# Moving z to token rows by VectorE block transposes and a DRAM round trip, in a two-stage transformer and mixture-of-experts kernel

## Chip, cores and metric

One core of one Trainium2 chip. The metric is the device time of the program in microseconds (us), the median of several runs; smaller is better.

## What is computed

Eight sequences x of 512 tokens by 256 channels go through four layers of a block, are added to the input and normalised, and then go through a gated mixture of eight experts with another residual and normalisation. All in fp32.

```python
def block(h, p):
    r = _retention(h, wk)
    m = r @ w1 + b1
    a, gate = jnp.split(m, 2, axis=-1)
    m = a * jax.nn.silu(gate) @ w2 + b2
    m = _groupnorm1(m, gg, gb)
    y = m + h
    f = jax.nn.gelu(y @ wf1 + bf1_, approximate=False) @ wf2 + bf2_
    return (_layernorm(f + y, lg, lb), None)
x = _layernorm(x + _L0_attn_ref(x, ...), axis=-1)
x = _layernorm(x + _L0_ffn_ref(x, ...), axis=-1)
```

The sum f + y, before its layernorm, is what the kernel calls z.

## The kernel before

**Work and stages.** The first stage is the four layers: 4 layers times 4 pairs of sequences give 16 steps. In a step two sequences, A and B, are in two slots with buffers and four PSUM banks each. The second stage (experts) follows from about 1060 us on and is not touched.

**Layout.** Most tensors of a sequence lie transposed, with channels on partitions: two chunks (c = 0, 1) of 128 channels by 512 tokens. The layernorm needs rows of tokens: four blocks of 128 tokens by 256 channels. fp32 products are done as three matmuls of a high half and a low half (mm3); ScalarE (ACT) rounds the high half from PSUM or SBUF, and VectorE (DVE) subtracts it for the low half. So a matmul phase is followed by the chain ACT high, DVE low, and the next matmul phase waits for the low half.

**Order.** The order of work on each engine is written out by hand in the functions `body`. The two slots are half a step apart: `body` of step `now` does A's and B's attention of this step, and in between the rest of B's, and the end of A's, of the step `before`. On TensorE (PE) the order is: A's `transpose_h`; B's `gated_projection`; A's `project_t`; `transpose_z(A)` (line 1945, eight transposes of 128x128 of y into two banks); B's `out_projection`; A's `scores`, with B's one-column `group_moments` (L1908) between; `retain(A)`; B's `up_projection` (first chunk L1922 and L1925); `transpose_r(A)`; projections and down projections; `project_t(B)`; `group_moments(A)`; `transpose_z(B)`; `scores(B)`; `up_projection(A)`; `retain(B)`; and so on.

**z.** DVE's `residual` (L1319) adds the down projection to y, in place: y is z then, channels on partitions. PE's `transpose_z` brings it to token rows in PSUM, ACT's `keep_z` (L923, two instructions) copies it to the SBUF tile z. DVE takes the statistics (`layernorm_stats`, L1327, and `layernorm_var`, L1336 to L1339), GpSimd (POOL) the inverse root (L661), ACT normalises (L936), POOL applies gain and bias (L388, L395) into h_out. The next user is `store_h` on the SP queue, which stores h_out to DRAM (L460) for the next layer; `load_h` (L456) loads it four steps later, and so h_in comes back through DRAM anyway.

**Chains around the change.** B's `scores` wait for both chunks of `low_t` (L1188, tu_sp from PSUM). The `group_moments` feed `groupnorm_var` (L1281), POOL's inverse root (L656) and `groupnorm_out`: gained (L1292), summed (L1297, writes y), ACT's `high_y` (L902), DVE's `low_y` (L1188, ry_sp), and then `up_projection`. B's `out_projection` waits for `low_u` (L1188, tu_sp from tmp), chunk c outer and chunk k inner. DVE's end of `body` is: `low_p(B)`, statistics of B's z, two `divide` (L1233 to L1237), `low_r(B)` (ry_sp from PSUM), which the first matmul of the next step's `gated_projection(B)` needs. All DMAs of this stage are issued by SP, in order, each behind its waits.

```python
def transpose_z(s, at, first=0):
    pe.wait_ge(z_ready[s], at.base + U)
    for k in range(TB):
        for c in range(DC):
            to = (k % 2) * D + c * P
            ins = nc.tensor.transpose(bank(s, first + k // 2)[:, to:to + P], y[s][:, c, cols(k)], ident[:, :])
```

Of the kernel before, what the change touches and what calls it, by code (L numbers as in the profile page):

```python
# [21 lines left out]
F32 = mybir.dt.float32  # L22
# [5 lines left out]
P = 128  # L28
EPS = 1e-5
# [21 lines left out]
def network(nc, x, xT, WkqvT, Wm1, Wm2, Wf1, Wf2, layer_cols, ln_g, ln_b,  # L51
            Wr, br, W1, W2, expert_cols, score_floor, out, h_store, folded, gate_rows, prepared):
# [30 lines left out]
    h_v = h_store.rearrange("i s (k p) d -> i s p k d", p=P)  # L83

# [20 lines left out]
    with ExitStack() as ctx:  # L105
# [146 lines left out]

        held = sem("held")
# [9 lines left out]
        def split_count(name, layer):  # L263
            return layer * len(SPANS) + list(SPANS).index(name) + 1

# [15 lines left out]
        zT_psum, z_kept, h_new = sems("zT_psum"), sems("z_kept"), sems("h_new")  # L281
# [23 lines left out]
        end_shift, end_half = sem("end_shift"), sem("end_half")  # L305

# [97 lines left out]
        def _(sp):  # L404
# [56 lines left out]

            def step(it, load, seam=None):
# [59 lines left out]
            for s in range(SLOTS):  # L522
                sp.sem_inc(h_stored[s], DMA)
            load_part(0, 0, kq_loaded)
# [298 lines left out]
        def _(act):  # L823
            for s in range(SLOTS):
                act.sem_inc(z_kept[s], U)
# [93 lines left out]
            def keep_z(s, at):  # L919
                act.wait_ge(h_new[s], at.base + U)  # L920
                for i in range(2):
                    act.wait_ge(zT_psum[s], at.base + 2 * i + 2)
                    nc.scalar.activation(z[s][:, 2 * i:2 * i + 2, :].rearrange("p k d -> p (k d)"), bank(s, i),  # L923
                                         ACT.Copy).then_inc(z_kept[s], 2)

            def keep_z_end():
                for i in range(2):
                    act.wait_ge(zT_psum[B_], LAST_STEP.base + 2 * i + 2)
                    nc.scalar.activation(z_end[:, 2 * i:2 * i + 2, :].rearrange("p k d -> p (k d)"), bank(B_, 2 + i),
                                         ACT.Copy).then_inc(z_kept[B_], 2)  # L930
# [89 lines left out]
            def body(now, before, seam, last=False, entry=False):  # L1020
# [13 lines left out]
                if before:  # L1034
                    keep_z(A_, before)
                else:
# [42 lines left out]
                if before:  # L1079
                    keep_z(B_, before)  # L1080
                else:
# [37 lines left out]
            keep_z(A_, LAST_STEP)  # L1119
# [12 lines left out]
            for w in range(QUADS):  # L1132
# [7 lines left out]
                if w == 0:  # L1140
                    keep_z_end()
# [38 lines left out]
        def _(dve):  # L1180
# [58 lines left out]
            def gated(s, at, c):  # L1239
                dve.wait_ge(m_psum[s], at.base + 2 * c + 2)  # L1240
# [76 lines left out]
            def residual(s, at, c):  # L1317
# [3 lines left out]
                    op0=ALU.add, op1=ALU.add).then_inc(z_ready[s], 2)  # L1321
# [262 lines left out]
            def body(now, before, seam, last=False, entry=False):  # L1584
# [3 lines left out]
                if seam:  # L1588
                    dve.wait_ge(z_ready[A_], before.base + U)
# [9 lines left out]
                if before:  # L1599
                    gated_products(B_, before)  # L1600
# [32 lines left out]
                if seam:  # L1633
                    dve.wait_ge(z_ready[B_], before.base + U)
# [5 lines left out]
                groupnorm_out(A_, now)  # L1640
                low_p(B_, now, range(TB))
                if before:
# [3 lines left out]
                for half in range(2):  # L1646
                    divide(B_, now, half)
# [124 lines left out]
        def _(pe):  # L1772
# [65 lines left out]
            def scores(s, at, blocks):  # L1838
                for b in blocks:
                    q = slice(LO[b], S)  # L1840
                    if b == 2:
                        pe.wait_ge(z_kept[s], at.base + U)
                    for k in range(DC):
                        pe.wait_ge(t_lo[s], at.base + 2 * k + 2)
                        ins = mm3(score_bank(s, b)[:, q], both(hT_sp[s], ALL, k, cols(b)), both(tu_sp[s], ALL, k, q),
                                  k == 0, k == DC - 1)
                    ins.then_inc(s_psum[s], 1)
# [30 lines left out]
            def out_projection(s, at):  # L1878
                w = weight("m2", DC)
                pe.wait_ge(w_lo, split_count("m2", at.layer))  # L1880
# [6 lines left out]
            def out_projection_end():  # L1887
                w = weight("m2", DC)
                for k in range(DC):
                    pe.wait_ge(u_lo[B_], LAST_STEP.base + 2 * k + 2)  # L1890
                    for c in range(DC):
# [330 lines left out]
```

## Time and profile before

| | |
|---|---|
| median of 3 runs | 2432.38 us (2432.0 to 2432.49) |
| profiled execution | 2433.66 us |
| its span in the trace | 2431.9 us (1.76 us lie around it) |
| mean granted TensorE clock | 0.996 of full speed |
| busy: PE / PE weight loads / DVE / ACT / POOL | 99% / 83% / 64% / 56% / 56% |

Times in a timeline are start and duration in us from the start of the span. An operation's start to the next one's start is its pitch; the ends of matmuls are modelled, so for PE the pitch is what counts. "[0.16 <-ACT ...]" is the idle time before the instruction and what ended it. In the rows of DMA queues a queue's packets, its MB and the time of its packets as a share of 16 engines are given for the window asked.

### The profile page before, as it was taken

What the parts mean: (1) busy time and instruction counts of PE and PEld (TensorE: products, weight loads), DVE (VectorE), ACT (ScalarE), POOL (GpSimd) and SP (SyncE); (2) the same over time, 40 slices, a digit from 0 to 9 for tenths busy, and PEclk for the clock granted to TensorE, in tenths of its full rate; (3) what the DMA queues carried; (4) which work ended last, traced back from release to release, by engine and by line L of the source; (5) the groups of instructions that cost most, each with busy time, mean ns of one, the idle gap of its engine ahead of it and who ended that gap; (6) DMA issues with size and microseconds to landing.
All of it is one profiled execution on the core that took longest, in us unless ns stands there. A gap on an engine that the chain in (4) does not pass through costs nothing. (4 is left out here: it accounts for less than half of the span.)

```text
span 2431.9 us, 35189 instructions
## 1 busy us (share of the span) xinstructions
PE 2403.9 (99%) x11662; PEld 2010.3 (83%) x11662; DVE 1547.7 (64%) x2876; ACT 1366.8 (56%) x2402; POOL 1357.4 (56%) x1255
## 2 busy tenths in 40 slices
PE   8999999999999999999999999999999999999998
PEld 6888888888888888887888888888888888888886
DVE  3566666666666666768787856665646756464545
ACT  4666766667666666666655644444444444444443
POOL 2355654455544644667888955546645556554444
PEclk9999999999999999999999999999999999999999
DMA  7011121111100112127655554544445443444442
GB/s 249 29 52 43 35 78 35 34 35 36 62 23 26 36 44 70 36 83 237 237 196 191 195 207 156 186 152 149 148 169 186 160 152 138 156 155 169 152 161 74
DMA packets 106823, 287.64 MB, mean 118 GB/s; under 512 B 7361, under 2 KB 77249, under 8 KB 90305
## 3 DMA queue, kind: packets, MB, share of 16 engines
q1 hardware_dynamic: 106128, 285.69, 33.7%
q8 instruction: 68, 1.11, 0.2%
q14 instruction: 67, 0.54, 0.1%
q10 hardware_dynamic: 560, 0.30, 0.0%
HBM read 216.36 MB, written 69.60 MB: 118 GB/s over the span
## 5 line engine op out<-in xcount | busy, mean ns | idle before, releaser
L701 POOL TENSOR_TENSOR hid_lo<-full,hid_hi 128x512 fp32r<-128x512 f32 x384 | 505.1, 1330 | 513.6 <-ACT full L1000 461.4
L1496 DVE SCALAR_TENSOR_TENSOR full<-ps,bias_cols,sum 128x512 f32<-128x512 f32 x384 | 288.2, 750 | 217.2 <-PE ps L1777 198.4
L1775 PE MATMUL ps<-hid_hi,m_w 128*128 128x512 f32 x1024 | 401.8, 392 | 0.1
L1777 PE MATMUL ps<-hid_hi,m_w 128*128 128x512 f32 x1024 | 398.8, 389 | 0.0
L1776 PE MATMUL ps<-hid_lo,m_w 128*128 128x512 f32 x1024 | 398.5, 389 | 0.0
L997 ACT ACTIVATE hid_hi<-ps,bias_cols 128x512 fp32r<-128x512 f32 x128 | 88.3, 690 | 496.4 <-PE ps L1777 496.4
L1775 PE MATMUL ps<-te_hi,m_w 128*128 128x512 f32 x896 | 351.5, 392 | 1.8 <-DVE sum L1483 0.9
L1777 PE MATMUL ps<-te_hi,m_w 128*128 128x512 f32 x896 | 349.3, 390 | 0.0
L1776 PE MATMUL ps<-te_lo,m_w 128*128 128x512 f32 x896 | 348.9, 389 | 0.0
L1777 PEld LDWEIGHTS ps<-hid_hi,m_w 128*128 128x128 f32 x1024 | 192.2, 188 | 40.4
L1775 PEld LDWEIGHTS ps<-hid_hi,m_w 128*128 128x128 f32 x1024 | 192.3, 188 | 39.5 <-issue 0.5
L1776 PEld LDWEIGHTS ps<-hid_lo,m_w 128*128 128x128 f32 x1024 | 192.4, 188 | 38.8
L1004 ACT ACTIVATE hid_hi<-full 128x512 fp32r<-128x512 f32 x256 | 161.7, 632 | 101.5 <-DVE full L1496 101.5
L1775 PEld LDWEIGHTS ps<-te_hi,m_w 128*128 128x128 f32 x896 | 168.3, 188 | 41.8 <-DVE sum L1483 4.0
L1777 PEld LDWEIGHTS ps<-te_hi,m_w 128*128 128x128 f32 x896 | 168.3, 188 | 35.4
L1776 PEld LDWEIGHTS ps<-te_lo,m_w 128*128 128x128 f32 x896 | 168.4, 188 | 34.2
L1483 DVE TENSOR_TENSOR sum<-ps,sum 128x512 f32<-128x512 f32 x128 | 88.2, 689 | 139.8 <-PE ps L1777 129.5
L633 POOL TENSOR_TENSOR pf_sp<-tmp,pf_sp 128x512 fp32r<-128x512 f32 x128 | 164.1, 1315 | 21.6 <-ACT pf_sp L910 21.6
L649 POOL TENSOR_SCALAR_AFFINE_SELECT pf_sp<-pf_sp 128x128 fp32r<-128x128 f32 x256 | 65.1, 293 | 193.9 <-DVE pf_sp L1188 193.7
L714 POOL TENSOR_TENSOR m_acc<-m_acc,out_scaled 128x512 f32<-128x512 f32 x125 | 169.3, 1354 | 1.3 <-DVE out_scaled L1513 1.3
L1487 DVE TENSOR_TENSOR sum<-ps,sum 128x512 f32<-128x512 f32 x128 | 88.1, 688 | 117.8 <-PE ps L1777 117.7
L1005 ACT ACTIVATE full<-full 128x512 f32<-128x512 f32 x256 | 159.1, 621 | 0.0
(210 smaller groups left out, 5593.2 us busy)
## 6 DMA issues: line engine op xcount, KB each, us to landing
m_w<-prepared SPq DMA_DIRECT2D x96, 1408.0 KB, 5.9
prepared<-m_w SPq DMA_DIRECT2D x32, 1408.0 KB, 5.8
h_store<-h_out SPq DMA_DIRECT2D x32, 512.0 KB, 3.2
we_raw<-in_W SPq DMA_DIRECT2D x64, 256.0 KB, 6.4
gate_bc<-gate_rows SPq DMA_DIRECT2D x64, 256.0 KB, 6.2
h_in<-h_store SPq DMA_DIRECT2D x24, 512.0 KB, 4.3
hT_in<-in_xT SPq DMA_DIRECT2D x8, 512.0 KB, 3.7
h_in<-in_x SPq DMA_DIRECT2D x8, 512.0 KB, 4.9
```

The source lines that it names most:

```text
L633: nc.gpsimd.tensor_tensor(out=lo, in0=full, in1=f32(hi), op=ALU.subtract).then_inc(done, n)
L701: nc.gpsimd.tensor_tensor(out=hid_lo[:, k, :], in0=full[:, k, :], in1=f32(hid_hi[:, k, :]), op=ALU.subtract).then_inc(hid_ready, 1)
L714: nc.gpsimd.tensor_tensor(out=at, in0=at, in1=out_scaled[:, j, :], op=ALU.add).then_inc(acc_added, 1)
L997: nc.scalar.activation(hid_hi[:, k, :], src, ACT.Relu, bias=bias)
L1004: nc.scalar.activation(hid_hi[:, k, :], src, ACT.Relu)
L1005: nc.scalar.activation(full[:, k, :], src, ACT.Relu).then_inc(relu_ready, 1)
L1483: nc.vector.tensor_tensor(out=sum2[:, :], in0=bank_b, in1=sum1[:, :], op=ALU.add).then_inc(sums, 1)
L1487: nc.vector.tensor_tensor(out=sum3[:, :], in0=bank_b, in1=sum1[:, :], op=ALU.add).then_inc(sums, 1)
L1496: nc.vector.scalar_tensor_tensor(out=full[:, k, :], in0=src, scalar=b1_col(e, 2 * fp + BLOCK_ROW[k]), in1=other[:, :], op0=ALU.add, op1=AL ...
L1775: nc.tensor.matmul(out, w[0], x[0], start=first, stop=False, skip_group_check=True)
L1776: nc.tensor.matmul(out, w[0], x[1], start=False, stop=False, skip_group_check=True)
L1777: return nc.tensor.matmul(out, w[1], x[0], start=False, stop=last, skip_group_check=True)
```

## The change

All steps but the last one's z (30 of 32 times): `transpose_z` on PE and `keep_z` on ACT are gone. In their place DVE transposes 32x32 blocks of y into tmp (`turn_z`, once for each chunk), and SP runs `move_z`: four DMAs of 128 KB each, one for each 32 partitions, whose runs in DRAM are 32 floats (128 bytes) long, a wait until they have landed, and one DMA of 512 KB back into z. The order of SP's queue changes, `gated` waits for the four stores because it overwrites tmp, and the statistics of B's z move behind the two `divide`. On PE `out_projection` now takes chunk k outer and chunk c inner, and B's scores begin with all that needs chunk 0 alone. In the last step z goes by PE as before.

```diff
+        z_blocks = z_store.rearrange("s (n a) (c q b) -> s q a c n b", a=BLOCK, b=BLOCK, c=DC)
+        def turned_z(s):
+            return tmp[s][:, 0:DC, :]
+        Z_STORE, Z_MOVE = P // BLOCK * DMA, (P // BLOCK + 1) * DMA
+        def residuals(s, c):
+            return (1, 2)[c] if s == A_ else (1, 3)[c]
...
             def load_h(s, it):
+                sp.wait_ge(h_stored[s], (it - PAIRS + 2) * DMA)
                 sp.wait_ge(hT_psum[s], it * U)
                 sp.wait_ge(h_lo[s], it * U)
-                sp.wait_ge(h_stored[s], (it - PAIRS + 2) * DMA)
...
+            def move_z(s, it):
+                done, moved = count(it * U + U), count(it * Z_MOVE + Z_MOVE + Z_STORE)
+                sp.wait_ge(z_ready[s], done)
+                for q in range(P // BLOCK):
+                    sp.dma_start(z_blocks[s, q], turned_z(s)[q * BLOCK:(q + 1) * BLOCK, :, :].rearrange("p c (n b) -> p c n b", b=BLOCK)
+                                 ).then_inc(z_moved[s], DMA)
+                sp.wait_ge(z_moved[s], moved)
+                sp.wait_ge(h_new[s], done)
+                sp.dma_start(z[s][:, :, :], z_v[s]).then_inc(z_moved[s], DMA)
...
-                for s in range(SLOTS):
+                def load_next(s):
                     load(s, it + 1)
                     if load is load_x:
                         load_xT(s, it + 1)
+                def finish(s):
                     store_h(s, it - 1)
                     if seam is not None:
                         load_lnv(s, seam)
+                move_z(A_, it - 1)
+                load_next(A_)
+                move_z(B_, it - 1)
+                finish(A_)
+                load_next(B_)
+                finish(B_)
...
+            move_z(A_, STEPS - 2)
             sp.wait_ge(m2_psum[A_], DONE)
             load_weights(0)
             sp.wait_ge(y_ready[A_], DONE)
             load_weights(1)
+            move_z(B_, STEPS - 2)
...
             def gated(s, at, c):
+                if c == 0:
+                    dve.wait_ge(z_moved[s], at.it * Z_MOVE + Z_STORE)
...
+            def turn_z(s, at, c):
+                dve.wait_ge(z_ready[s], at.base + residuals(s, c))
+                nc.vector.transpose(turned_z(s)[:, c, :], y[s][:, c, :]).then_inc(z_ready[s], 1)
             def layernorm_stats(s, at, blocks, at_z=None):
-                dve.wait_ge(z_kept[s], at.base + 2 * U)
+                    dve.wait_ge(z_moved[s], at.it * Z_MOVE + 2 * Z_MOVE)
...
-                    gated_products(B_, before)
+                    gated_products(B_, before, lambda part: turn_z(A_, before, part))
...
                     residual(B_, before, 0)
+                    turn_z(B_, before, 0)
...
-                groupnorm_out(A_, now)
+                groupnorm_out(A_, now, lambda part: before and part == 0 and turn_z(B_, before, 1))
                 low_p(B_, now, range(TB))
+                for half in range(2):
+                    divide(B_, now, half)
                 if before:
                     for blocks in HALVES:
                         layernorm_stats(B_, before, blocks)
                     layernorm_var(B_, before)
-                for half in range(2):
-                    divide(B_, now, half)
...
+            def scores_by_chunk(s, at, before):
+                for b in (0, 2, 3):
+                    score(s, at, b, 0, before)
+                score(s, at, 0, 1, before)
+                scores(s, at, (1,), before)
+                for b in (2, 3):
+                    score(s, at, b, 1, before)
...
-                for c in range(DC):
-                    for k in range(DC):
-                        pe.wait_ge(u_lo[s], at.base + 2 * k + 2)
+                for k in range(DC):
+                    pe.wait_ge(u_lo[s], at.base + 2 * k + 2)
+                    for c in range(DC):
                         ins = mm3(bank(s, OUT[c]), both(w, ALL, k, cols(c)), both(tu_sp[s], ALL, k), k == 0, k == DC - 1)
-                    ins.then_inc(m2_psum[s], 2)
+                        if k == DC - 1:
+                            ins.then_inc(m2_psum[s], 2)
...
                 if before:
-                    transpose_z(A_, before)
                     out_projection(B_, before)
...
-                if before:
-                    transpose_z(B_, before)
-                else:
+                if not before:
                     pe.wait_ge(fold_out, 3 * (L - 1))
-                scores(B_, now, range(TB))
+                scores_by_chunk(B_, now, before)
```

## Rows read from the trace of the kernel before

**Rows 1.** The page: busy time of the engines, and the chain's shares by engine.

```profile
PE 2403.9 (99%) x11662; PEld 2010.3 (83%) x11662; DVE 1547.7 (64%) x2876; ACT 1366.8 (56%) x2402; POOL 1357.4 (56%) x1255
...
PE 42%; DVE 0%; ACT 0%; issue 0%; POOL 0%; DVEq 0%; ACTq 0%
```

**Rows 2.** Windows, one step: length; busy of PE, weight loads, DVE, ACT, POOL; clock; DMA.

```profile
705.70:770.40 64.70, 64.62 (x355) 55.55 (x353) 41.91 (x101) 42.93 (x79) 31.88 (x37) 1.00 0.10 32
```

**Rows 3.** The tile y: the matmul records of transpose_z; duration in ns.

```profile
L1945 PE MATMUL ps<-ident,y x256: 270/272/329, 83.5 to 1090.1; 128*128 128x128 f32 x128
```

**Rows 4.** Timeline of PE, the half of a step that begins with A's transpose_h.

```profile
725.93 0.48 PE L1775 MATMUL ps<-ry_sp,w_fold 128*128 128x512 f32 x1
...
734.20 1.03 PE L1945 MATMUL ps<-ident,y 128*128 128x128 f32 x8
734.99 0.48 PE L1775 MATMUL ps<-tu_sp,w_plain 128*128 128x512 f32 x1
735.30 0.39 PE L1776 MATMUL ps<-tu_sp,w_plain 128*128 128x512 f32 x1
...
740.24 0.28 PE L1908 MATMUL ps<-gin,mean_w 128*128 128x4 f32 x2
...
745.67 2.11 PE L1922 MATMUL ps<-ry_sp,w_plain 128*128 128x512 f32 x8
```

**Rows 5.** Timeline of PE, the other half, about transpose_z of B.

```profile
704.81 1.07 PE L1945 MATMUL ps<-ident,y 128*128 128x128 f32 x8
705.64 0.47 PE L1775 MATMUL ps<-tu_sp,hT_sp 128*128 128x512 f32 x1
...
709.54 2.06 PE L1922 MATMUL ps<-ry_sp,w_plain 128*128 128x512 f32 x8
...
712.35 0.44 PE L1775 MATMUL ps<-ry_sp,w_plain 128*128 128x512 f32 x1
```

**Rows 6.** Timeline of DVE over both halves.

```profile
709.37 0.69 DVE L1188 TENSOR_TENSOR ry_sp<-y,ry_sp 128x512 fp32r<-128x512 f32 x1 [0.16 <-ACT ry_sp L902]
...
711.55 0.69 DVE L1188 TENSOR_TENSOR ry_sp<-y,ry_sp 128x512 fp32r<-128x512 f32 x1 [0.83 <-ACT ry_sp L902]
...
719.31 0.17 DVE L1237 RECIPROCAL den<-den 128x2 f32<-128x2 f32 x1
723.22 1.29 DVE L1188 TENSOR_TENSOR ry_sp<-ps,ry_sp 128x512 fp32r<-128x512 f32 x2 [3.75 <-ACT ry_sp L888]
...
730.59 1.88 DVE L1188 TENSOR_TENSOR tu_sp<-tmp,tu_sp 128x512 fp32r<-128x512 f32 x1 [0.83 <-ACT tu_sp L898]
...
738.02 0.70 DVE L1265 BATCH_NORM_STATS2 gstat<-ps 128x6 f32<-128x512 f32 x1 [0.16 <-PE ps L1777]
...
739.62 0.16 DVE L1273 SCALAR_TENSOR_TENSOR gin<-gsm,gmv 128x2 f32<-128x2 f32 x1
```

**Rows 7.** Timeline of ACT: A's high_t, and B's high_y.

```profile
735.28 1.07 ACT L872 ACTIVATE tu_sp<-ps 128x512 fp32r<-128x512 f32 x2
...
744.79 0.63 ACT L902 ACTIVATE ry_sp<-y 128x512 fp32r<-128x512 f32 x1 [1.58 <-DVE y L1297]
```

**Rows 8.** Timeline of POOL: the inverse root of B's z, and a later bias.

```profile
720.61 1.01 POOL L661 TENSOR_TENSOR zr<-zr,neg_half 128x4 f32<-128x4 f32 x1
...
729.52 2.40 POOL L395 TENSOR_TENSOR h_out<-z,lnv 128x1024 f32<-128x1024 f32 x1 [0.23 <-POOL z L388]
```

**Rows 9.** DMA issues: count, KB each, median us from issue to landing.

```profile
h_store<-h_out SPq DMA_DIRECT2D x32, 512.0 KB, 3.2
...
h_in<-h_store SPq DMA_DIRECT2D x24, 512.0 KB, 4.3
```

**Rows 10.** DMA queues from 727 to 732 us: one store and one load of h.

```profile
q1 hardware_dynamic: 1056, 1.05, 66.0%
```

**Rows 11.** DMA queues from 2 to 4 us: ACT's queue, loading small constants.

```profile
q10 hardware_dynamic: 246, 0.03, 10.4%
```

**Rows 12.** DMA queues from 1116 to 1117.6 us: the store of gate_rows.

```profile
q1 hardware_dynamic: 80, 0.03, 8.5%
```

**Rows 13.** DMA queues from 936 to 937 us: small loads behind large ones.

```profile
q1 hardware_dynamic: 620, 0.29, 115.7%
```

More of the change, by code:

```diff
@@ L28 @@
 P = 128
+BLOCK = 32
 EPS = 1e-5
@@ L51, in network @@
 def network(nc, x, xT, WkqvT, Wm1, Wm2, Wf1, Wf2, layer_cols, ln_g, ln_b,
-            Wr, br, W1, W2, expert_cols, score_floor, out, h_store, folded, gate_rows, prepared):
+            Wr, br, W1, W2, expert_cols, score_floor, out, h_store, z_store, folded, gate_rows, prepared):
     B, S, D = x.shape
@@ L917, in hidden, with keep_z_end @@
                     high_f(s, at, c - 1)
-            def keep_z(s, at):
-                act.wait_ge(h_new[s], at.base + U)
+            def keep_z_end(s):
+                if s == A_:
+                    act.wait_ge(h_new[A_], LAST_STEP.base + U)
+                at_z, first = (z[A_], 0) if s == A_ else (z_end, 2)
                 for i in range(2):
[L922 to L930, printed above, removed]
+                    act.wait_ge(zT_psum, U * s + 2 * i + 2)
+                    nc.scalar.activation(at_z[:, 2 * i:2 * i + 2, :].rearrange("p k d -> p (k d)"), bank(s, first + i),
+                                         ACT.Copy).then_inc(z_kept, 2)
             def normalise_z(s, at, at_z=None):
@@ L1078, in body @@
                 high_t(B_, now)
-                if before:
-                    keep_z(B_, before)
-                else:
+                if not before:
                     act.wait_ge(fold_stored, (L - 1) * DMA)
@@ L1118, in _ @@
             high_u(B_, LAST_STEP, 1)
-            keep_z(A_, LAST_STEP)
+            keep_z_end(A_)
             act.wait_ge(consts_loaded, 5 * DMA)
@@ L1588, in body @@
                 if seam:
-                    dve.wait_ge(z_ready[A_], before.base + U)
+                    dve.wait_ge(z_ready[A_], before.base + residuals(A_, 1))
                     hold(dve, held)
@@ L1836, in project_t, with score, scores @@
                 ins.then_inc(t_psum[s], 2)
-            def scores(s, at, blocks):
+            def score(s, at, b, k, before):
+                q = slice(LO[b], S)
+                if k == 0 and b >= 2 and before:
+                    pe.wait_ge(z_ready[s], before.base + residuals(s, b - 2))
+                pe.wait_ge(t_lo[s], at.base + 2 * k + 2)
+                ins = mm3(score_bank(s, b)[:, q], both(hT_sp[s], ALL, k, cols(b)), both(tu_sp[s], ALL, k, q), k == 0, k == DC - 1)
+                if k == DC - 1:
+                    ins.then_inc(s_psum[s], 1)
+            def scores(s, at, blocks, before):
                 for b in blocks:
-                    q = slice(LO[b], S)
-                    if b == 2:
-                        pe.wait_ge(z_kept[s], at.base + U)
                     for k in range(DC):
[L1844 to L1847, printed above, removed]
+                        score(s, at, b, k, before)
+            def scores_by_chunk(s, at, before):
[5 more added lines that the diff above has]
+                    score(s, at, b, 1, before)
             def retain(s, at):
@@ L1879, in out_projection @@
                 w = weight("m2", DC)
-                pe.wait_ge(w_lo, split_count("m2", at.layer))
-                for c in range(DC):
-                    for k in range(DC):
-                        pe.wait_ge(u_lo[s], at.base + 2 * k + 2)
-                        ins = mm3(bank(s, OUT[c]), both(w, ALL, k, cols(c)), both(tu_sp[s], ALL, k), k == 0, k == DC - 1)
-                    ins.then_inc(m2_psum[s], 2)
[L1887 to L1891, printed above, removed]
-                        ins = mm3(bank(B_, OUT[c]), both(w, ALL, k, cols(c)), both(tu_sp[B_], ALL, k), k == 0, k == DC - 1)
+                if at is not LAST_STEP:
+                    pe.wait_ge(w_lo, split_count("m2", at.layer))
+                for k in range(DC):
+                    pe.wait_ge(u_lo[s], at.base + 2 * k + 2)
+                    for c in range(DC):
+                        ins = mm3(bank(s, OUT[c]), both(w, ALL, k, cols(c)), both(tu_sp[s], ALL, k), k == 0, k == DC - 1)
                         if k == DC - 1:
-                            ins.then_inc(m2_psum[B_], 2)
+                            ins.then_inc(m2_psum[s], 2)
             def down_projection_end():
@@ L2061, in body @@
                     fold_vm(0)
-                scores(A_, now, (0, 1))
+                scores(A_, now, (0, 1), before)
                 if before:
                     group_moments(B_, before)
-                scores(A_, now, (2, 3))
+                scores(A_, now, (2, 3), before)
                 if not before:
@@ L2096, in body @@
                 group_moments(A_, now)
-                if before:
-                    transpose_z(B_, before)
-                else:
+                if not before:
                     pe.wait_ge(fold_out, 3 * (L - 1))
-                scores(B_, now, range(TB))
+                scores_by_chunk(B_, now, before)
                 up_projection(A_, now)
@@ L2122, in _ @@
             pe.wait_ge(consts_loaded, 5 * DMA)
-            out_projection_end()
+            out_projection(B_, LAST_STEP)
             product(0, 0)
@@ L2183, in build @@
     network(nc, x, xT, WkqvT, Wm1, Wm2, Wf1, Wf2, layer_cols, ln_g, ln_b, Wr, br, W1, W2, expert_cols, score_floor,
-            out, h_store, folded, gate_rows, prepared)
+            out, h_store, z_store, folded, gate_rows, prepared)
 def laid_out(inputs):
```

25 lines of the change are left out of this document (15 added, 10 removed).

## The prediction

> **What bounds the kernel now.** I read the page first, then one step by windows, then PE's timeline against the other engines'. The page has PE busy for 99% of the span and nearly all of the chain that ended last is PE's [rows 1]. Busy time alone is no proof, so the window of one step is next: of 64.70 us PE is busy 64.62 [rows 2]. PE hardly ever waits, DVE and ACT have a third of the step free and POOL half. Taking work off PE is therefore the right direction; the question is whether what PE would then wait for is close behind. That is in the timelines: they show for each wait of PE how long before PE's arrival the awaited result was there. These margins are mostly far below what is removed.
>
> **PE, the removed transposes.** A set of eight takes from 734.20 to 734.99, 0.79 us, and the matmul behind it has a pitch of 0.31 instead of the 0.23 of its kind [rows 4]; in the other half it is 0.83 [rows 5]. So 0.87 us a set. Each record lasts 272 ns, but they overlap, so the pitch counts [rows 3]. Of the 32 sets 30 go (15 bodies with a step before, two each): 26.1 us if nothing takes their place. ACT's 60 copies of keep_z go too; ACT is not what PE waits for where they stood (its next work waits for the scores), so I count nothing.
>
> **A's half: most is kept.** Behind the transposes stands B's out_projection. It needs the low half of chunk 1 of u, on DVE right before (the op at 730.59 is chunk 0's [rows 6]). With k outer PE asks for chunk 1 after six matmuls (1.36 us) instead of three (0.68), which gives back 0.68 of the 0.87. I find it in time by about 0.3 us. The next stop is group_moments(B) at 740.24 [rows 4]. It needs gin, ready at 739.78 (739.62 + 0.16), and the second statistics in front of it (738.02) waited for PE and comes 0.24 earlier at most, because the first follows low_t(A), which hangs on ACT's high_t(A) at 735.28 [rows 6, 7]. So gin is ready at 739.54 and PE can be there at 739.4: the moments come about 0.6 earlier. The chain from there (POOL's root, groupnorm_out, high_y) ends with high_y at 745.42 (744.79 + 0.63), and PE's L1922 at 745.67 follows at once [rows 4, 7]: it is bound by that chain already, and gains the same 0.6. It gains the full 0.87 if high_t(A) comes earlier. That hangs on the op at 730.59: it took 1.88 us and not 0.69, because it ended only 0.55 after POOL's bias, which ran from 729.52 to 731.92 [rows 6, 8]. If POOL's work shifts, this block can vanish or move. I take 0.75, ends 0.3 and 0.87.
>
> The turns of A's z lie in gated_products(B), where DVE idles 0.83 before each low_u [rows 6]. The price of a turn of 128x512 isn't in the trace. The nearest rows: two DVE instructions of 128x512 in a row last 1.29 and one 0.69, so a pitch of 0.60 [rows 6]. Below that no fp32 pass of 512 columns in these rows lies; above I take twice as much, 1.2. At 0.6 both are hidden; at 1.2 each low_u is late by 0.4, and A's half keeps 0.3. The Trainium skill (SBUF — State Buffer, Who interferes with whom) says that a DVE instruction with two SBUF inputs and a GpSimd one block each other, and one with a single SBUF input outside the 2-port modes does not. The stretched op has two SBUF inputs and agrees; by that rule a turn is never held up by POOL, and the 0.6 stands.
>
> **B's half: the gain turns into a loss.** After the moments PE now goes at once to scores(B). Chunk 0 of low_t is nearly in time, and the order by chunk lets PE work 1.3 us before it needs chunk 1, which it needed after 0.7. So the scores start some 0.6 earlier than 705.64 [rows 5]. But what follows is L1922 at 709.54, which waits for high_y(A) that was done 0.2 before, and then L1775 at 712.35, which waits for low_y of chunk 1: it started at 711.55 and ended at 712.24, 0.1 before PE [rows 5, 6]. This chain starts at the moments and goes through DVE; the transposes stood behind the moments, so taking them out does not make it earlier. PE's saved 0.87 is waited away at these two places. And the turn of B's chunk 1 is put into this chain, in front of low_y of chunk 0 at 709.37, where DVE was idle for 0.16 only [rows 6]: 0.6 less 0.16 makes the chain 0.4 later. B's half gets longer by 0.4 (by 1.0 at the upper price of a turn). The turn of B's chunk 0, before low_hT(B), has over 1 us of margin: nothing.
>
> **The DMAs, on SP.** move_z issues five DMAs, each some 0.4 us of queue time, and SP stands still twice. Behind it are load_h and store_h. Both have tens of us: h_in is used most of a step later, h_out four steps later. Nothing, unless a round trip takes over 20 us. The four stores have 4096 runs of 128 bytes, 256 on each of 16 engines. No row has this run as a store. Loads of small constants: 10.4% of 16 engines times 2 us over 246 packets is 13.5 ns each, at about 120 bytes [rows 11]. Runs of 1 KB: 66.0% of 80 us over 1056 is 50 ns [rows 10]. The one store with shorter runs than 1 KB, 80 packets in 8.5% of 25.6 us, is 27 ns, at 512 bytes [rows 12]. That small runs are fed fast enough is seen up to 620 packets in a us [rows 13], so 4096 in 6.6 us or less. I take 20 ns, between the first and the last: 5.1 us; ends 3.5 (13.5 ns) and 12.8 (50 ns). Landing: h_store takes 3.2 us for 32 packets of 50 ns on each engine (1.6), so 1.6 is fixed; the load back is 4.3 [rows 9]. Round trip 5.1 + 1.6 + 4.3 + 0.4 of issue = 11.4 us.
>
> A's z is turned at about 734 and its statistics are taken 24 us later: hidden. B's z is turned at about 709.9 and back at 721.3. The statistics stand behind the second divide, at 719.5, and need 2.1 us; then low_r(B) must be done with its first half 0.1 before 725.93 [rows 4, 6], thus start by 725.1, and the statistics by 722.9. Margin 1.6 us, which a packet price of 26 ns uses up. Below it the cost is nothing on PE. On POOL B's root moves from 720.61 to about 723.5 [rows 8] and pushes both layernorm outputs back 3 us; POOL is free enough for that, and mask_scores(A) at about 741 is still met. This shift is what moves the block of low_u in A's half.
>
> **Sum.** A's half −0.75, B's half +0.4: −0.35 a step, 15 times, −5.2 us. The seams and the last step (there B's move_z stands behind two weight loads, some 1 to 3 us late once) are within the range. Profiled 2433.66 − 5.2 = 2428.4; the median of the runs is 1.28 below the profiled time, so 2427.2.
>
> **Rivals.**
> - **PE gets it all.** If both chains give way (the turn fits in, POOL's shift frees low_u), 30 x 0.87 goes: 2406. For it: PE is busy all the time. Against: the margin of 0.1 at 712.35 [rows 5, 6]. Partial forms, 0.7 to 1.7 us a step, give 2422 to 2406. Chance 0.15.
> - **B's z comes back late (slower).** Place: layernorm_stats(B), with low_r(B) queued behind it on DVE and PE's gated_projection(B) behind that. It decides from 26 ns a packet on. At 32 ns the round trip is 8.2 + 1.6 + 4.3 + 0.4 = 14.5 us, z is there at 724.4 and PE stands 1.5 us a step: 15 x (1.5 − 0.35) = +17, 2449. At 50 ns it is 19.1 us, 6.1 us a step, +86: 2518. For it: the short store in rows 12 costs 27 ns at least. Against: loads of the same size cost half of it. The Trainium skill (DMA: Bandwidth & Descriptors, Specifications) says that below 512 bytes the engine does read-modify-write and is off its line rate. If that doubles the 13.5 ns, it is 27 ns and just past the point. Chance 0.23.
> - **The chains cost more than I read.** A turn of 0.8 to 1.2 us, or POOL's shift blocking the second low_u: −0.3 in A's half, +0.6 to +1.0 in B's: +4 to +10 us: 2436 to 2443. Chance 0.12.
> - My forecast (−0.1 to −0.65 a step, 2422.5 to 2431): chance 0.5.
>
> **How the numbers follow.** 0.2% of this kernel, about 4.9 us, is what a measurement can tell from no change. The forecast's centre lies just at it; I give 0.28 of its 0.5 to faster, 0.22 to the same. The first rival is faster (0.15). Of the second 0.03 is the same, of the third 0.04, the rest slower. Faster 0.43, same 0.29, slower 0.28. The range reaches down to 2410 (most of the first rival) and up to 2450 (the second up to 32 ns).
>
> **What would show it.** No L1945 but for the last step. At scores(B) a short wait for low_t; waits of PE for high_y and low_y in B's half, together about what was removed, with low_y of chunk 1 0.4 later after the moments; moments(B) about 0.6 to 0.9 earlier in the step. The turn at 0.7 us. Stores of z landing within 8 us and DVE's statistics of B at 721 to 722 by the step's count. I am wrong if DVE idles before these statistics past 722.9 and PE waits for ry_sp of low_r(B); or if the chain from the moments to low_y is not what ends B's half.

## The result, and the profile after

The changed kernel takes 2441.2 us (median of 5 runs, 2439.8 to 2441.7) where the kernel before takes 2432.0 (5 runs, 2429.8 to 2432.5): ratio 1.0038, interval 1.0027 to 1.0049. It is **slower by 9 us**, 0.38%; the forecast was 2427.2. The profiled execution took 2441.28, 1.8 more than its span. In one run of experiment 10 the granted clock was 0.758 and the time 2928.7 us; it is left out, and every other run had 0.993 or more.

The page after, busy time and chain, answering [rows 1]:

```profile
PE 2389.5 (98%) x11422; PEld 1985.1 (81%) x11422; DVE 1575.6 (65%) x2936; ACT 1336.0 (55%) x2342; POOL 1356.4 (56%) x1255
...
PE 42%; DVE 0%; ACT 0%; issue 0%; POOL 0%; DVEq 0%; ACTq 0%
```

PE has 240 matmuls and 14 us of busy time less, as it should, in a span that is 7.6 us longer. The window from 150 to 1060 us, which lies in the transformer steps, of the kernel before and then of the one after (length; busy of PE, weight loads, DVE, ACT, POOL; clock; DMA share; GB/s):

```profile
150.00:1060.00 910.00, 903.48 (x4899) 774.09 (x4897) 604.92 (x1434) 610.43 (x1104) 478.18 (x525) 1.00 0.13 42
```

```profile
150.00:1060.00 910.00, 882.65 (x4639) 745.51 (x4638) 624.33 (x1481) 577.53 (x1040) 480.48 (x524) 1.00 0.29 74
```

At the same granted clock PE stands idle for 27.3 us instead of 6.5. What it stands for is in the list of waits, 60 to 1074 us (total, times, longest):

```profile
PE ps L1775 <- DVE tu_sp L1188: 5.3, 8, 1.1
PE ps L1908 <- DVE gin L1273: 1.4, 2, 0.9
PE ps L1922 <- ACT ry_sp L902: 0.3, 1, 0.3
```

```profile
PE ps L1814 <- DVE tu_sp L1216: 11.8, 15, 1.4
PE ps L1966 <- ACT ry_sp L938: 5.2, 14, 0.9
PE ps L1952 <- DVE gin L1303: 4.5, 11, 1.0
PE ps L1814 <- DVE ry_sp L1216: 3.0, 3, 2.4
PE ps L2056 <- DVE m_xs L1408: 2.7, 1, 2.7
```

The first block is before, the second after. Three waits are old ones grown: the low half of t or u, the groupnorm's input, and the high half of y. The last two are new (m_xs is the normalised x of the second stage).

**Where in a step.** To place them I cut the trace at the starts of group_moments, called moments(A) and moments(B) here: moments(A) to moments(B) is one interval, the one in which the z of both sequences was transposed; moments(B) to moments(A) of the next step is the other, and hardly changed (sum 434.5 before, 435.1 after). The first one, in us:

```
step    1     2     3     4     5     6     7     8     9     10    11    12    13    14    15
before  35.51 35.62 35.46 36.61 35.85 35.58 39.11 36.65 35.81 35.57 35.59 36.64 35.44 35.51 36.12
after   36.90 36.99 35.73 37.49 34.90 34.86 38.37 37.45 36.40 34.86 35.72 36.07 36.20 36.19 41.79
```

Two things are seen. The last step alone loses 5.7. And the inner steps have two values: some gain 0.6 to 0.95 (5, 6, 7, 10, 12), others lose 0.6 to 0.9 (4, 8, 9, 13, 14) with the very same instructions: steps 5 and 9 are the same place in two layers, 34.90 and 36.40. Steps 1 and 2 lose 1.4 each. Steps 9 and 10 after, first POOL and then DVE, about low_u(B,0), the low half of chunk 0 of B's u:

```profile
664.82 2.41 POOL L400 TENSOR_TENSOR z<-z,lnv 128x1024 f32<-128x1024 f32 x1
667.46 2.39 POOL L407 TENSOR_TENSOR h_out<-z,lnv 128x1024 f32<-128x1024 f32 x1 [0.23 <-POOL z L400]
...
730.41 2.42 POOL L400 TENSOR_TENSOR z<-z,lnv 128x1024 f32<-128x1024 f32 x1
733.06 2.93 POOL L407 TENSOR_TENSOR h_out<-z,lnv 128x1024 f32<-128x1024 f32 x1 [0.23 <-POOL z L400]
```

```profile
666.55 0.70 DVE L1356 STREAM_TRANSPOSE tmp<-y 128x512 f32<-128x512 f32 x1
667.46 2.93 DVE L1216 TENSOR_TENSOR tu_sp<-tmp,tu_sp 128x512 fp32r<-128x512 f32 x1 [0.21 <-ACT tu_sp L934]
...
732.13 0.70 DVE L1356 STREAM_TRANSPOSE tmp<-y 128x512 f32<-128x512 f32 x1
733.04 0.69 DVE L1216 TENSOR_TENSOR tu_sp<-tmp,tu_sp 128x512 fp32r<-128x512 f32 x1 [0.21 <-ACT tu_sp L934]
```

Both come just when POOL is between B's gain (L400) and B's bias (L407). In step 10 DVE starts 0.02 us ahead and POOL's bias is the one held (2.93); in step 9 both print as 667.46, POOL is ahead by 8 ns in the trace's records, and low_u lasts 2.93 instead of 0.69. In the kernel before the bias had already been running for 1.07 us when the same low_u(B,0) started (729.52 and 730.59 in [rows 6, 8]), which made it 1.88 there and 1.6 to 1.9 in the other steps from 4 to 14, but for the seams' neighbours 7 and 11. The Trainium skill (SBUF — State Buffer, SBUF: two separate sides) says that whichever of the two starts first has the shared ports for its whole instruction; these rows agree. The turn, one SBUF input, ran beside POOL's gain in 0.70 both times. In steps 1 and 2 the block lies elsewhere, on the two operations of low_hT(B) from hT_in: 5.14 and 5.24 us from start to end, where the kernel before has 4.04 and 4.13.

The new operations themselves answer to the prices asked for in the prediction. The tile view of the turn (times, then ns least/median/most), the page's DMA issues, and the queue while the stores run, 712.3 to 714.5 us (packets, MB, share of 16 engines):

```profile
L1356 DVE STREAM_TRANSPOSE tmp<-y x60: 692/700/714, 78.8 to 1036.7; 128x512 f32<-128x512 f32 x60
```

```profile
z_store<-tmp SPq DMA_DIRECT2D x120, 128.0 KB, 3.3
z<-z_store SPq DMA_DIRECT2D x30, 512.0 KB, 3.9
```

```profile
q1 hardware_dynamic: 1513, 0.19, 56.2%
```

0.562 x 16 x 2.2 us over 1513 packets is 13.1 ns for a store of 128 bytes.

The last step, before and after (DVE, with SP's queue of after between):

```profile
1038.70 1.39 DVE L1327 BATCH_NORM_STATS2 zstat<-z 128x6 f32<-128x256 f32 x4
...
1044.33 4.53 DVE L1370 TENSOR_SCALAR m_xs<-m_xs,m_mv,m_rstd 128x256 f32<-128x256 f32 x8
```

```profile
1038.69 0.37 SPq L511 DMA_DIRECT2D we_raw<-in_W  x1
1039.11 0.47 SPq L513 DMA_DIRECT2D we_raw<-in_W  x1
1039.62 3.30 SPq L482 DMA_DIRECT2D z_store<-tmp  x4
1045.39 0.37 SPq L486 DMA_DIRECT2D z<-z_store  x1
```

```profile
1049.66 1.41 DVE L1365 BATCH_NORM_STATS2 zstat<-z 128x6 f32<-128x256 f32 x4 [2.24 <-DMA z<-z_store]
...
1051.78 6.91 DVE L1408 TENSOR_SCALAR m_xs<-m_xs,m_mv,m_rstd 128x256 f32<-128x256 f32 x8
```

B's z is late here, the only time in the kernel that DVE waits for it, and eight normalisations of x and low_r(B) queue behind it. The normalisations last 6.91 us instead of 4.53; POOL's root, gain and bias (1052.02 to 1058.55) now run beside them, where before they began at their end (the gain at 1048.88).

### The profile page after: what moved, and what is told of

Same layout as the page of the kernel before. It is cut to its first block and busy times, and to the rows that moved or that the text cites. A ratio compares the mean times of both kernels' runs of the same rounds, so it can differ in the third digit from the quotient of the medians.

```text
span 2439.5 us, 34910 instructions
## 1 busy us (share of the span) xinstructions
PE 2389.5 (98%) x11422; PEld 1985.1 (81%) x11422; DVE 1575.6 (65%) x2936; ACT 1336.0 (55%) x2342; POOL 1356.4 (56%) x1255
## 5 line engine op out<-in xcount | busy, mean ns | idle before, releaser
L1816 PEld LDWEIGHTS ps<-te_hi,m_w 128*128 128x128 f32 x896 | 168.3, 188 | 35.5
```

The lines of the kernel that those rows point to most:

```text
L1816: return nc.tensor.matmul(out, w[1], x[0], start=False, stop=last, skip_group_check=True)
```

## Experiments

All times below are medians against the kernel before on the same chip (2431.2 to 2432.1 there). "Last interval" and "steps 0 to 14" are sums of the intervals defined above, of each kernel's profiled execution; before they are 36.12 and 539.5, after 41.79 and 542.2.

**1. The last step: statistics of B's z behind low_r(B).** On the changed kernel, in the last body:

```diff
-                if before:
+                if before and not last:
                     for blocks in HALVES:
                         layernorm_stats(B_, before, blocks)
                     layernorm_var(B_, before)
                 if last:
                     for t in range(2):
                         normalise_x1(0, t)
                 low_r(B_, now)
+                if last:
+                    for blocks in HALVES:
+                        layernorm_stats(B_, before, blocks)
+                    layernorm_var(B_, before)
```

> The changed kernel, but in the last step alone VectorE takes the statistics of B's z behind low_r(B) and not in front of it. My theory: of the changed kernel's 7.6 us of longer span, 5.7 lie between the last two group_moments (41.79 us from A's to B's, 36.12 before), because VectorE stood 2.24 us for z (its DMAs are queued behind two weight loads on SP), then ran the normalisation of x beside POOL (6.91 us for eight operations, 4.53 before), and low_r(B) came behind both. So this interval falls to 36 to 37 us and the kernel gets 5 to 6 us faster than the changed one: 2435 to 2436. Rival: PE waits there for the normalised x or for the weights because the new DMAs share the engines; then moving the statistics gains under 1 us and it stays at 2440 to 2441.

Measured: 2439.3 (1.0032, 1.0020 to 1.0045). The last interval is 39.71: 2.1 of the 5.7 come back, not all. The wait for m_xs is gone, but DVE now has this where it had 1.62 us in the kernel before:

```profile
1056.71 3.81 DVE L1389 TENSOR_TENSOR m_w<-we_raw,m_w 128x1408 fp32r<-128x1408 f32 x1
```

It stands ahead of gated(B,1), and POOL's gain and bias of A's z, which ended at 1053.8 before, run until 1059.0 here. PE waits 2.8 us for the tu_sp behind it. With the statistics taken behind low_r(B), POOL's root comes as late as in the changed kernel (1052.46 against 1052.02), so its work now lies on the next long DVE instruction.

**2. The order of the statistics alone.** On the kernel before, B's statistics moved behind the divisions, as in the change, and nothing else.

```diff
-                if before:
-                    for blocks in HALVES:
-                        layernorm_stats(B_, before, blocks)
-                    layernorm_var(B_, before)
                 for half in range(2):
                     divide(B_, now, half)
+                if before:
+                    for blocks in HALVES:
+                        layernorm_stats(B_, before, blocks)
+                    layernorm_var(B_, before)
```

> The kernel before, with one edit of the change alone: the statistics of B's z stand behind the two divides on VectorE. TensorE still transposes z, there are no turns and no new DMAs. My theory: in the changed kernel POOL's inverse root of B's z starts 17.3 us after A's moments instead of 15.9, because the statistics stand behind the divides, and this alone moves POOL's gain and bias of 2.4 us each against VectorE's low_u, which then is blocked for 2.1 us in some steps and not in others. So here too low_u has durations of 0.7 in some steps and 2.5 to 2.9 in others, and where it is long the interval from A's moments to B's is over 36 us; in the last step the normalisation of x meets POOL and takes some 2 us longer. In all +2 to +10 us over the kernel before: 2434 to 2442. Rival: the loss comes from the turns, the DMAs or the new order on PE; then this kernel is within 1.5 us of before.

Measured: 2435.1 (1.0013, 1.0004 to 1.0022). Steps 0 to 14 are 541.8 (+2.3), the last interval 37.33 (+1.2). Without any turn or DMA this order makes a part of the loss: steps 1 and 2 are 36.7 and 36.8, nearly the 36.9 and 37.0 of after, and low_hT(B) lasts 5.21 and 5.32 there. Low_u(B,0) is free (0.69) in seven of the steps 1 to 14 (4, 5, 6, 8, 9, 10, 12), and not one of them is faster than before by over 0.05. In steps 13 and 14 it lasts 2.88, and they lose 0.5. That A's transposes, which TensorE does meanwhile, are what covers the shorter block is argued from this and from the turned kernel, where a free low_u does shorten the step.

**3 and 4. B's gain and bias elsewhere on POOL.** From the head of POOL's step to just before rstd_group(A), on the changed kernel and on the one before (all but the last step and the seams, the steps in which a new layer begins; SP's store_h of B comes one step later, and SP's loops are written out):

```diff
-                if earlier:
+                if earlier and (seam or last):
                     layernorm_out(pool, nc.gpsimd, B_, earlier)
                 split_h(A_, now)
...
+                if earlier and not (seam or last):
+                    layernorm_out(pool, nc.gpsimd, B_, earlier)
                 rstd_group(A_, now)
```

> The changed kernel, with POOL's gain and bias of B's z moved from the start of a step's body to the 7 us in which POOL is idle before A's second inverse root (in the 10 bodies that are not the first two of the stage, a layer's first or the last), and B's store of h and the load of the layernorm's gain behind it on SP; SP's loops are written out. My theory: in these 10 bodies low_u of B takes 0.7 to 1.3 us in each, and the interval from A's moments to B's falls to what the unblocked steps of the changed kernel have: 34.9 (34.0 to 34.1 in the first layer's, 36.0 at a new layer's): together 8 to 11 us less than the changed kernel, 2430 to 2433. Rival: what is late in the slow steps is late because of VectorE's own turns between the gated products; then low_u stays in its two kinds and the time stays at 2440 to 2441.

> The kernel before with the same move of POOL's gain and bias and of SP's store. My theory: its low_u of B is blocked for 1.1 to 1.2 us in nearly every step, but its PE arrives later, behind the transposes, so little is lost there: 0 to 3 us faster than before, 2429 to 2432. Rival: the block costs the kernel before as much as the changed one; then it gets 8 us or more faster, and the change would still be a loss beside it.

Measured: 2443.5 (1.0045, 1.0031 to 1.0058) and 2438.4 (1.0026, 1.0017 to 1.0035). Both expectations failed. The two values of the inner steps did become one, 35.5 to 35.6, but the block was only moved: scores(B) now starts 1.08 to 1.17 after moments(A) instead of 0.34. POOL's bias (704.46, 2.39) runs beside a tiny DVE operation of A's groupnorm ahead of moments(A) and low_t(B), which takes 0.16 in the changed kernel:

```profile
704.70 2.16 DVE L1307 TENSOR_TENSOR gin<-gmv,lc 128x2 f32<-128x2 f32 x1
```

So neither of the two places tried on POOL is free; the work has to leave POOL for its price to be seen.

**5 and 6. B's gain and bias on VectorE.** DVE idles up to 5.7 us behind low_r(A), waiting for A's gate. On the changed kernel (with experiment 1's edit) and on the kernel before, both with SP's later store_h of B as in 3 and 4:

```diff
                 low_r(A_, now)
+                if earlier and not (seam or last):
+                    layernorm_out(dve, nc.vector, B_, earlier)
```

> The changed kernel with two edits: B's gain and bias of z (two POOL operations of 2.4 to 2.9 us each) run on VectorE behind low_r(A), in the gap of some 5.7 us in which it waits for A's gate, instead of at the head of POOL's step; and in the last body B's statistics stand behind low_r(B). Theory 'POOL's operations block low_u(B)': with POOL's two operations gone from beside it, moments(A) to moments(B) is 34.7 to 35.0 in nearly all steps (36.2 to 37.5 in the blocked steps of the changed kernel), 8 to 10 us in sum, and the last step gives 2; total 2427 to 2431. Rival 'the turned path has a dearer chain that POOL has no part in': the intervals stay where they were and the total is 2438 to 2442. Rival 'VectorE's own share makes up for it': the two operations fill the gap and delay gated(A) or POOL's split of h(B) and f(B); moments(B) to moments(A) grows from 29.15 by 1 or more and the total is 2440 or above.

> The kernel before with B's gain and bias of z on VectorE behind low_r(A) in place of POOL. Here TensorE has the 16 transposes of the step to do while low_u(B) waits, and an unblocked low_u(B) showed no gain where the statistics of B were late. Theory: same as before within 3 us (2429 to 2434), so that the move is worth 8 to 10 us only with z off TensorE. Rival 'any kernel gains from POOL's relief': 4 to 8 us faster than before (2424 to 2428), and the change then still loses by as much beside it.

Measured: 2431.7 (1.0001, 0.9992 to 1.0010) and 2430.5 (0.9994, 0.9985 to 1.0003). The first is 7.6 us under experiment 1, which differs by this edit and by what goes with it on POOL and SP. Its steps 5, 6, 9, 10 and 13 are all 34.92 to 34.94, steps 0 to 14 sum to 534.0 (540.7 in experiment 1), and moments(B) to moments(A) grew by 0.8 in all. Steps 1 and 2 are 2.4 and 0.8 shorter than in experiment 1, steps 4, 8 and 13 are 1.3 to 1.4 shorter each. In the kernel before the same edit is worth 1.5 us, within the interval. DVE does in 3.2 us what takes POOL 4.8:

```profile
745.22 1.21 DVE L400 TENSOR_TENSOR z<-z,lnv 128x1024 f32<-128x1024 f32 x1
746.64 2.03 DVE L407 TENSOR_TENSOR h_out<-z,lnv 128x1024 f32<-128x1024 f32 x1 [0.20 <-DVE z L400]
...
751.03 0.75 DVE L1276 SCALAR_TENSOR_TENSOR tmp<-ps,lc,tmp 128x512 f32<-128x512 f32 x1 [2.36 <-ACT tmp L933]
```

and 2.36 us of the gap are left. So B's gain and bias on POOL cost about 7 us with z off TensorE and about 2 with the transposes in place. Low_u(B,0) is not free of POOL in either kernel: POOL's split of h(B) now comes earlier and lies on it (1.49 in experiment 5, 1.60 in experiment 6). In the turned kernel a hold of this size costs nothing that can be seen: the changed kernel's steps with a free low_u are 34.86 to 34.90.

**7 and 8. One sequence of the pair at a time.** The changed kernel with B's z back on TensorE (transposes, copies, early statistics, B's scores in the old order), and the mirror, with A's z back:

```diff
-                move_z(B_, it - 1)
...
-                scores_by_chunk(B_, now, before)
+                transpose_z_B(before)
+                scores(B_, now, range(TB), before)
```

```diff
-                move_z(A_, it - 1)
...
+                    transpose_z_A(before)
                     out_projection(B_, before)
```

> The changed kernel with only image A's z turned by VectorE and moved over DRAM; B's z is transposed by TensorE and kept by ScalarE as in the kernel before, with B's statistics ahead of the divisions and B's scores in their old order. Theory (A's part gains 0.7 a step where low_u(B) is free; the losses come from B's late statistics, which shift POOL's root of B's z by 1.4 us, and from B's z in the last step): last interval 36 to 36.5 in place of 41.8, the others as before less 0 to 0.7; total 2423 to 2430, faster than before. Rival 'A's part is no gain either, since low_u(B) now collides with POOL where TensorE's transposes had covered it': 2431 to 2436. Rival 'the loss is in A's turn or its DMA': 2438 or more.

> The mirror of the kernel with only A's z turned: here B's z is turned by VectorE and moved over DRAM with all that belongs to it (late statistics, B's scores by chunk), A's z is transposed by TensorE and kept by ScalarE in its old place. Theory 'B's part alone is the loss': the two parts add up, so that this is 2431.9 plus the 9.2 of the change plus the 6.2 that A's part gains, 2443 to 2450. The last interval is near 41.8, moments(A) to moments(B) elsewhere is like the kernel before plus 0 to 2. Rival 'the loss is a meeting of the two' (two copies on one queue, or POOL's block of ten microseconds only harms where A's transposes are gone from beside low_u(B)): 2434 to 2440.

Measured: A alone 2425.8 (0.9979, 0.9969 to 0.9989), B alone 2447.0 (1.0064, 1.0050 to 1.0078). They add up: −6.2 and +15.8 make +9.6, and the change has +9.2. A alone keeps the last interval at 36.12 and takes the steps from 539.5 to 532.1. B alone was profiled in its fastest execution, 2442.5; it has 42.52 in the last interval, and 546.3 in the steps: retain(B) starts 0.28 to 0.38 later after moments(A) than before in each of the steps 1 to 14, steps 1, 2 and 8 lose 0.9 to 1.4, most others 0.3.

**9. The orders of PE.** The changed kernel with the out projection output by output and B's scores block by block:

```diff
-                for k in range(DC):
-                    for c in range(DC):
+                for c in range(DC):
+                    for k in range(DC):
...
-                scores_by_chunk(B_, now, before)
+                scores(B_, now, range(TB), before)
```

> The changed kernel with the out projection and B's scores in their old orders (output by output, block by block). Theory: the orders are worth 0 to 0.7 us a step, since by chunk the first product starts when the first half of low_u is there: in steps with a late low_u half both orders wait for the second chunk, and by output the first half of the work is not hidden; scores of B by block wait 0.1 to 0.6 us more for the second chunk of low_t. Sum 3 to 12 us slower than the changed kernel (2444 to 2453). Rival 'the orders do nothing': 2441 within 2. Rival 'the chunk orders hurt': under 2439.

Measured: 2443.4 (1.0047, 1.0033 to 1.0060) where the change has 1.0038: the two can't be told apart, and the second account is the nearest. Step 10 is 34.88 to 34.86. Two steps of the profile are longer with the old orders: step 1 is 38.56 instead of 36.90, step 4 is 38.63 instead of 37.49; step 9 is 34.86 instead of 36.40, since DVE came first there. Whether the orders or the chance of one execution made the first two longer is not shown.

**10. The rest of the last step.** On experiment 5, the first subtraction of the experts' weights behind low_u(B,1):

```diff
             low_u(B_, LAST_STEP, 0)
-            low_weights(0)
             gated(B_, LAST_STEP, 1)
             sum_tokens(0, 0)
             low_u(B_, LAST_STEP, 1)
+            low_weights(0)
```

> The kernel with B's gain and bias on VectorE and the last body's statistics behind low_r(B), and one edit more: VectorE's first subtraction of the experts' weights (3.81 us there, 1.62 in the kernel before, since POOL's gain and bias of A's z run beside it), on which TensorE's 2.8 us wait for B's second tu_sp hangs, stands behind low_u(B,1) instead of ahead of gated(B,1). Theory 'the last step's rest is this block': last interval 36.4 to 37.2 in place of 39.5, total 2427 to 2430. Rival 'the expert's first product waits for the weights instead': the interval falls but the stretch behind moments(B) grows by as much, total 2431 to 2433.

Measured: 2431.1 (0.9999, 0.9990 to 1.0009), against 2431.7 without the edit. The subtraction is back at 1.61 us, but the last interval only falls from 39.51 to 38.52, and PE waits 1.8 us for gin instead. So the rival's total holds, with another wait than the one it named. What the last step's remaining 2.4 us consist of is left open.

**11. Both findings together.** A's z turned, B's on TensorE, B's gain and bias on VectorE (the edits of 5 and 7).

> The kernel with only A's z turned, and B's gain and bias of z on VectorE behind low_r(A). Theory (with A's transposes gone, low_u(B)'s block of 1.7 to 1.9 and 1.1 us by POOL is what TensorE waits for in most steps): the intervals of 35.0 to 35.4 become 34.4 to 34.9, the sum 4 to 6 us less, total 2419 to 2423. Rival 'the block is still covered by the products of A, as in the kernel before with this same edit': 2424 to 2427.

Measured: **2419.2** (0.9950, 0.9936 to 0.9963; 2418.7 to 2420.4 in 5 runs), 12 us faster than the kernel before and the fastest of all. Steps 0 to 14 sum to 525.6. One of its steps:

```profile
693.58:757.49 63.91, 63.84 (x346) 54.79 (x345) 45.48 (x105) 42.02 (x76) 27.95 (x34) 1.00 0.18 49
```

PE is busy for 63.84 of 63.91 us, where [rows 2] had 64.62 of 64.70: the removed set of transposes, 0.79, has turned into time. Against experiment 6, which has the same gain and bias on DVE but both sets of transposes, steps 0 to 14 are 11.5 us shorter (537.1 there), 0.77 a step.

**12. The turn in the chain.** On experiment 5, B's second turn behind A's whole y chain:

```diff
-                groupnorm_out(A_, now, lambda part: before and part == 0 and turn_z(B_, before, 1))
+                groupnorm_out(A_, now)
+                if before:
+                    turn_z(B_, before, 1)
```

> The kernel with B's gain and bias on VectorE and the last body's statistics behind low_r(B) (its steps are free of the POOL block: 34.93 us), and one edit more: B's second turn of z (0.70 us) stands behind the whole of A's y chain instead of between gained(1) and low_y(0) of it. Theory 'the turn in the chain is what B's half costs in each step': up projection of A waits 0.3 to 0.6 us less, retain(B) starts 10.3 to 10.4 after moments(A) in place of 10.7, moments(A) to moments(B) 34.5 to 34.6, total 2426 to 2428 (2431.7 without the edit). Rival 'the chain is set by ScalarE's high half (its ry_sp is what TensorE waits for) and not by the turn': intervals within 0.1 of 34.93, total 2430 to 2433. Rival 'the later store makes B's z late for its statistics': low_r(B) waits, low_u(B) or moments(B) late by 0.5 or more, total above 2433.

Measured: 2456.7 (1.0097, 1.0081 to 1.0114), **25 us slower** for a turn that begins 3.0 us later (7.38 after moments(A) instead of 4.33). The first account is right on retain(B), the third on the time. Outside the seams retain(B) starts 10.35 to 10.39 after moments(A) instead of 10.70 to 10.74, so the turn did cost 0.35. But of DVE's waits, 60 to 1080 us, the one for z from the DMA has grown; experiment 5, then this one:

```profile
DVE zstat L1369 <- DMA z<-z_store: 1.0, 3, 0.4
```

```profile
DVE zstat L1369 <- DMA z<-z_store: 41.9, 14, 4.1
```

3.0 us in each of 14 steps, and behind the statistics stand low_r(B) and PE's gated_projection(B).

## Why the prediction was wrong

- **Price of a turn: right.** Pitch 0.6 from neighbours was assumed, a record of 0.7 expected; 60 turns took 692 to 714 ns and none was held by POOL.
- **Price of the DMA: right in kind, too dear.** Taken 20 ns a packet, ends 13.5 and 50; measured 13.1, just under the lower end. (Of the 80 packets of [rows 12], 16 are under 512 bytes, so 27 ns was an average and not the price of 512 bytes.) Back at 14.5 us after moments(A) (the load is issued at 717.42 and lands 3.9 later, from 706.82) where I had 16.6. For the Trainium skill's read-modify-write below 512 bytes (DMA: Bandwidth & Descriptors, Specifications) I had a rival in which the small load's price doubles; that doubling does not show: stores of 128 bytes cost what such loads cost. The rival "B's z comes back late" did not happen in 14 of 15 steps, but experiment 12 shows how near it was.
- **A's half, −0.75: right where POOL lets it.** A alone gains 7.4 us over steps 0 to 14, 0.5 a step, with B's gain and bias on POOL, and 0.77 a step with them on DVE in both kernels (experiment 11 against 6).
- **B's half, +0.4: near.** B alone makes retain(B) 0.28 to 0.38 later; taking the turn out of the chain gives 0.35 back (experiment 12).
- **The sum −5.2: not met.** Steps 0 to 14 got 2.7 longer. With B's gain and bias off POOL (experiment 5) they sum to 534.0, −5.5 against before; the nearness to −5.2 is chance in part, since the same move gives 2.4 without the change, and against experiment 6 only 3.1 are left.
- **The step that failed** is the last sentence of the part on DMA: "POOL is free enough for that … This shift is what moves the block of low_u in A's half". The root of B's z moved, by 1.4 us and not 3 (17.3 after moments(A) instead of 15.9), and took with it four operations in a row, from 725.43 to 735.95. I priced a moved block as a chance of gain within −0.3 to −0.87; it was an exposed one. In the kernel before, POOL's bias was well under way when low_u(B,0) came (1.88 of [rows 6]), and a free low_u(B,0) would have gained nothing (experiment 2). After, gain and bias meet low_u(B,0) at the bias's very start: it lasts 0.69 or up to 2.93, and the long one costs 1.5 (step 9: 36.40, and 34.87 in experiment 1, where DVE came first). In steps 1 and 2 they hold low_hT(B) for 1.1 longer. B's gain and bias on POOL cost about 7 us in all (experiment 5 against 1), where I had put the shift at nothing or better; this is nearly the whole of the 7.9 between −5.2 and +2.7.
- **The last step** was put at 1 to 3 us "within the range" and left out of the sum. It cost 5.7. I had counted the delay of z (2.24 us of DVE's time), not what queues behind its statistics on DVE, nor POOL's work sliding beside it. With the statistics out of the way 2.1 come back (experiment 1); 2.4 are still open after experiment 10.
- The third rival, "the chains cost more than I read … POOL's shift blocking", is the nearest, with the wrong low_u named (the second; it is the first). It had 0.12. That its +4 to +10 holds the measured +9.2 is luck in part: it says nothing of the last step, which makes 5.7 of it.

## What to carry to other kernels

When work is taken off the engine that bounds, what stood beside it loses its cover: look for the stretched records (1.88 where the kind takes 0.69) in the profile of before and price each, and where it may move to, at full length. A delay of one small operation on an in-order queue must be followed to everything behind it, on that queue and on the engine that shares its ports. Where two halves are symmetric, price and try each alone: here one was worth 6 us and the other cost 16.

## What was not expected of the hardware

- A start 0.02 us ahead of POOL's (733.04 against 733.06) or 8 ns behind it (667.46) decides between 0.69 and 2.93 us for one DVE instruction. It falls either way from step to step of one execution, and from one execution to another: step 9 is blocked in the changed kernel's profile (36.40) and free in that of experiment 1 (34.87), whose edit touches the last step alone. A median hides this; the interval table does not.
- Runs of 128 bytes stored to DRAM cost 13.1 ns each. By this, 4096 of them are an estimated 3.4 us over 16 engines.
- The same multiplication of 128x1024 takes DVE 1.21 us (745.22 in experiment 5) and POOL 2.41 (664.82 in the changed kernel).
